# A recurrent-attention step with a new order on all five engines, its correction copied by ScalarE, and three expert sums in place of two

## The chip, the cores and the metric

The kernel runs on one core of one Trainium2 chip. The metric is device microseconds (us) for one execution. TensorE (PE) multiplies matrices into PSUM; VectorE (DVE) and ScalarE (ACT) read PSUM and SBUF; GpSimd (POOL) reads SBUF only; SyncE (SP) issues most of the DMAs. Each engine executes its own instructions in program order and waits on semaphores, so an instruction that waits holds up everything behind it on its engine.

## The reference

Two layers over 1024 tokens of width 256. The first is gated delta-rule attention (16 key heads, each with two value heads, all of size 128) and then a small MLP. The second is four-head softmax attention and then a mixture of 32 experts, four per token. What the change concerns:

```python
def step(state, xs):                      # per token, per value head
    q_t, k_t, v_t, g_t, b_t = xs
    state = state * jnp.exp(g_t)[..., None, None]
    kv = jnp.einsum('bhk,bhkv->bhv', k_t, state)
    delta = (v_t - kv) * b_t[..., None]
    state = state + jnp.einsum('bhk,bhv->bhkv', k_t, delta)
    out = jnp.einsum('bhk,bhkv->bhv', q_t, state)
...
mixed = jax.nn.silu(_causal_conv(mixed, conv_w))    # 4 taps, on q, k and v
o = o * jax.nn.silu(z); o = o * rsqrt(mean(o * o) + EPS) * norm_gamma
return o @ w_out
# experts: y[e] = (silu(x_e @ w_gate[e]) * (x_e @ w_up[e])) @ w_down[e]
# out[token] += weight * y[e][row of token]
```

## The kernel before

**The head steps.** `heads` computes the delta rule in chunks of 128 tokens: c = 0 to 7 for each key head. The program has 18 head steps, h = 0 to 17. Step h works on several heads at once: it scans head h-1, projects and convolves head h+1 (`p0` to `p7`, `base`, `tap`), inverts the chunk matrices of head h, and normalises and projects head h-2. Steps 2 to 14 are alike, with all of this work.

**One chunk of the scan** has three parts, (c, 0), (c, 1) and (c, 2). In part 0 PE multiplies the state S by keys (`ks`, L820) and queries (`qs`, L822), and DVE makes X from it (L1284). In part 1 PE multiplies X with the inverse Uf (`tx`, L833), and DVE copies the result from PSUM into Dl (L1289). In part 2 PE multiplies Dl with At (`o`, L839); ACT scales Dl into Dt (L1112); PE multiplies Dt with the keys (`su`, L845); DVE updates S (L1297) and finishes the output (L1309, L1311). So a chunk is a chain ks, X, tx, Dl, Dt, su, S that goes to and fro between the engines, and the next chunk starts from S.

**The order.** A step is a list of 23 quanta, the parts (0, 1), (0, 2), (1, 0) to (7, 2), numbered 0 to 22. Three tables written by hand, PE_PLAN, ACT_PLAN and DVE_PLAN, say which further work an engine does behind quantum k: the row `12: y6a/3 y6b/0` puts the products y6a and y6b behind quantum 12, into PSUM banks 3 and 0. Each engine runs its quantum and then its row, in this order:

```python
for h in STEPS:
    for k in range(NQUANTA):
        if h in SCAN:
            scan_quantum(h, *QUANTA[k])
        for name in dve_row(h, k):
```

SP and POOL have a fixed order per step, written as code.

**The inversion** goes around by HBM. PE makes key products (`kk0`, `kk1`, L799), ACT evicts them to `heads_kneg` (L1164), SP stores the 32x32 diagonal blocks to `kk_blocks` (L639, `key_block_stores`) and loads them regrouped into `heads_A` (L646, `load_key_blocks`). DVE computes block scales from it (`scales`, L1317 to L1325). POOL scales A (L1556) and eliminates in 31 rounds (L1566, L1569; `solve`). SP then stores the inverse (L734) and loads it into Uf (L742) in the next step, where DVE turns three blocks (`turn`, L1332); PE and ACT extend the inverse to 128 columns (`y6`, `u6`, `y7`, `u7`). POOL's rounds use the same tile as Y6 and start only when `u6a` is done.

**The experts** (`experts`, after everything else): PE computes expert e, DVE weights its 128 rows (L2252), POOL adds them with an indirect DMA into a sum in HBM (L2174). Adds to one sum follow each other, each waiting for the last to land; e alternates between SUMS = 2 sums. DVE's `places(e)` waits for the add of expert e-4. At the end SP loads the first sum in two halves (L2152) and the second in four quarters (L2156), DVE adds them to x (L2269, L2274), and SP stores x (L2161).

## Time and profile before

| | us |
|---|---|
| Median of 3 runs (lowest, highest) | 1622.71 (1614.81, 1622.80) |
| The profiled execution, its own time | 1607.9 |
| Its span in the trace | 1606.1 |
| Granted TensorE clock, mean, of full speed | 0.937 |
| Busy PE / DVE / ACT / POOL over the span | 1358.1 / 1028.1 / 757.8 / 749.6 |
| Steps 2 to 14, from 171.05 to 1075.91 | 904.86 |

Over the whole span PE is the busiest engine. A share of the span says little of what a stage waits for, so the rows below are taken from stages: from the 13 like steps, from one step (that with h = 10, from its first `tx` at 728.15 to the next step's at 797.04), and from the experts' end.

### The profile page before, as it was taken

Reading aid. Unit: us, or ns where it says so; the run is one execution under the profiler, and the core shown is the slowest. Engines: PE = TensorE matmul, PEld = TensorE weight load, DVE = VectorE, ACT = ScalarE, POOL = GpSimd, SP = SyncE. Lnnn points to the kernel's source line nnn. Section 1 sums busy time; section 2 is a strip of 40 time slices with the busy share of each in tenths; the row PEclk is TensorE's granted clock in tenths of the full one; section 3 lists DMA queues with packets and bytes.
Section 4 is the critical chain, followed back from the end, with each engine's and each line's share of the span. In section 5 each row is a group of like instructions: output and inputs, shape, how many; then the busy total and the mean of one; then the engine's idle time right before and its main releaser. Section 6 shows DMA issues by size and latency. Waiting matters only on the chain. (4 is left out here: it accounts for less than half of the span.)

```text
span 1606.1 us, 24958 instructions
## 1 busy us (share of the span) xinstructions
PE 1358.1 (85%) x8680; PEld 900.5 (56%) x8680; DVE 1028.1 (64%) x2086; ACT 757.8 (47%) x1787; POOL 749.6 (47%) x1226
## 2 busy tenths in 40 slices
PE   6686888979898897989889798898789689969994
PEld 3364655656565565656556565556554356644673
DVE  5765867778686777868777786776550256561353
ACT  3454645555554555555556564556442246311121
POOL 1774674746657474665747566472100000007254
PEclk9878999999999999999999999998999799979997
DMA  3513335444543444444344443435410390022387
GB/s 90 135 35 95 82 113 115 100 102 106 142 102 94 108 115 108 96 132 106 94 109 115 111 104 116 115 79 138 134 41 0 146 322 5 1 77 104 92 182 159
DMA packets 230989, 169.49 MB, mean 106 GB/s; under 512 B 163730, under 2 KB 200806, under 8 KB 228048
## 3 DMA queue, kind: packets, MB, share of 16 engines
q1 hardware_dynamic: 224720, 159.36, 36.9%
q0 software_dynamic: 6144, 8.53, 2.9%
q8 instruction: 70, 1.15, 0.3%
q14 instruction: 55, 0.45, 0.1%
HBM read 103.59 MB, written 64.65 MB: 105 GB/s over the span
## 5 line engine op out<-in xcount | busy, mean ns | idle before, releaser
L1273 DVE SCALAR_TENSOR_TENSOR heads_y<-psum_banks,gdn_conv_w,heads_y 128x1021 f32<-128x1021 f32 (+2 forms) x192 | 245.2, 1277 | 70.6 <-ACT heads_y L1087 69.0
L791 PE MATMUL psum_banks<-main_hT,gdn_w_in 128*128 128x512 f32 x512 | 265.8, 647 | 19.5 <-DVE heads_y L1273 13.1
L1566 POOL TENSOR_TENSOR heads_tmp<-heads_XT,heads_A 128x126 f32<-128x126 f32 (+22 forms) x496 | 189.1, 381 | 74.4 <-PE psum_banks L956 36.5
L1569 POOL TENSOR_TENSOR heads_XT<-heads_XT,heads_tmp 128x126 f32<-128x126 f32 (+22 forms) x496 | 200.9, 405 | 38.8
L1112 ACT ACTIVATE heads_Dt<-heads_Dl,heads_coef 128x128 f32<-128x128 f32 x224 | 77.6, 394 | 243.2 <-DVE heads_Dl L1289 242.8
L791 PEld LDWEIGHTS psum_banks<-main_hT,gdn_w_in 128*128 128x128 f32 x512 | 100.3, 208 | 114.8 <-issue 88.3
L1540 POOL TENSOR_TENSOR heads_og<-heads_og,heads_fac 128x512 f32<-128x512 f32 x60 | 60.5, 1039 | 144.8 <-DVE heads_fac L1343 144.8
L905 PE MATMUL psum_banks<-heads_w_z,main_hT 128*128 128x256 f32 x512 | 123.8, 386 | 0.0
L1105 ACT ACTIVATE heads_O<-psum_banks,heads_coef 128x128 f32<-128x128 f32 x224 | 69.9, 363 | 114.1 <-PE psum_banks L822 113.5
L2106 POOL DMA_INDIRECT expert_rows<-moe_rows,route_dest x32 | 31.4, 981 | 185.9 <-DVE route_dest L2085 176.5
L926 PE MATMUL psum_banks<-heads_ogT,heads_w_o 128*128 128x512 f32 x240 | 116.6, 608 | 1.0
L1123 ACT ACTIVATE heads_junk<-heads_og 128x128 f32<-128x128 f32 x256 | 78.0, 305 | 71.0 <-DVE heads_og L1311 66.5
L1551 POOL TENSOR_TENSOR heads_v_s<-heads_v_s,heads_k_root 128x2048 f32<-128x2048 f32 x16 | 58.2, 3638 | 98.5 <-DMA heads_v_s<-values_by_tokens 98.5
L905 PEld LDWEIGHTS psum_banks<-heads_w_z,main_hT 128*128 128x128 f32 x512 | 95.5, 194 | 11.4
L833 PEld LDWEIGHTS psum_banks<-heads_X,heads_Uf 128*128 128x128 f32 x448 | 63.5, 192 | 55.8 <-issue 28.7
L1289 DVE COPY heads_Dl<-psum_banks 128x256 f32<-128x256 f32 x128 | 53.1, 415 | 64.8 <-PE psum_banks L833 63.3
L1087 ACT ACTIVATE heads_y<-psum_banks,gdn_conv_w 128x1024 f32<-128x1024 f32 x64 | 71.4, 1116 | 43.0 <-PE psum_banks L791 42.7
L839 PE MATMUL psum_banks<-heads_Dl,main_lend 128*128 128x128 f32 x256 | 48.8, 319 | 48.0 <-DVE heads_Dl L1289 48.0
L833 PE MATMUL psum_banks<-heads_X,heads_Uf 128*128 128x128 f32 x448 | 74.1, 288 | 17.9 <-DVE heads_X L1284 17.6
L839 PE MATMUL psum_banks<-heads_Dl,heads_At 128*128 128x128 f32 x256 | 47.2, 310 | 48.6 <-DVE heads_Dl L1289 48.6
L845 PE MATMUL psum_banks<-heads_Dt,heads_k_tok 128*128 128x256 f32 x224 | 79.8, 441 | 4.5 <-ACT heads_Dt L1112 2.5
L820 PE MATMUL psum_banks<-heads_S,heads_kT 128*128 128x256 f32 x224 | 71.9, 403 | 10.9 <-DVE heads_S L1297 9.9
(280 smaller groups left out, 3002.8 us busy)
## 6 DMA issues: line engine op xcount, KB each, us to landing
values_by_tokens<-heads_v_s SPq DMA_DIRECT2D x64, 256.0 KB, 3.8
heads_v_s<-values_by_tokens SPq DMA_DIRECT2D x16, 1024.0 KB, 5.0
outputs_by_features<-heads_ogT SPq DMA_DIRECT2D x120, 128.0 KB, 2.3
heads_ogT<-outputs_by_features SPq DMA_DIRECT2D x30, 512.0 KB, 3.5
main_w_gu<-in_w_gu SPq DMA_DIRECT2D x4, 2816.0 KB, 20.8
gdn_w_in<-in_w_in SPq DMA_DIRECT2D x16, 512.0 KB, 4.4
heads_A<-kk_blocks SPq DMA_DIRECT2D x64, 128.0 KB, 2.6
keys_by_tokens<-heads_k_tok SPq DMA_DIRECT2D x64, 128.0 KB, 3.3
```

What stands on the lines that cost most here:

```text
L791: ins = pe.matmul(out[:, half * 512:(half + 1) * 512], w_in[:, kd_, j * P:(j + 1) * P], hT[:, kd_, half * 512:(half + 1) * 512], start=kd_ ...
L820: pe.matmul(flat(bank_a[:, 0:2]), kT[(h - 1) % 3][:, cs], flat(S[:]), start=True, stop=True).then_inc(a_full.sem, 1)
L833: ins = pe.matmul(bank_a[:, e], Uf[old][:, e * C + c], rhs, start=True, stop=True)
L839: ins = pe.matmul(bank_b[:, e], At[old][:, c * HD + e], Dl[:, e], start=True, stop=True)
L845: pe.matmul(flat(bank_a[:, 0:2]), k_tok[old][:, c], flat(Dt[:]), start=True, stop=True).then_inc(a_full.sem, 1)
L905: ins = pe.matmul(flat(bank[b][:, 2 * j:2 * j + 2]), hT[:, k, c * P:(c + 1) * P], w_z[:, k], start=k == 0, stop=k == KD - 1)
L926: ins = pe.matmul(flat(bank[b][:]), w_o[:, e, f], ogT[:, u // 2].rearrange("p q (c e) j -> p e c q j", e=HD)[:, e], start=e == 0, stop=e = ...
L1112: ins = act.activation(Dt[:, e], Dl[:, e], ACT.Copy, scale=coef[:, TAIL, h - 1, i:i + 1])
L1123: act.activation(junk[:], og[(h - 1) % 2][:, c * HD + e], ACT.Square, accum_out=ms[:, c * HD + e:c * HD + e + 1]).then_inc(sq_ready.sem, 1)
L1273: dve.scalar_tensor_tensor(y[j][:, shift:T], src[:, 0:T - shift], conv_w[:, head, j, t:t + 1], y[j][:, shift:T], ALU.mult, ALU.add).then_i ...
L1566: pool.tensor_tensor(tmp[:, 0:n, 0:m], bc_last(XT[:, 0:n, j], m), bc_mid(A0[:, j, j + 1:BLK], n), ALU.mult).then_inc(solve_step.sem, 1)
L1569: pool.tensor_tensor(XT[:, 0:n, j + 1:BLK], XT[:, 0:n, j + 1:BLK], tmp[:, 0:n, 0:m], ALU.add).then_inc(solve_step.sem, 1)
```

## The change

All tables of a steady step are filled anew, and the order of SP and of POOL becomes a table too, SP_PLAN and POOL_PLAN (POOL's order is the same as before). The PSUM banks of the four decay products are permuted, and some products change bank. The copy of the correction into Dl goes from DVE to ACT, in quantum part 1; ACT then makes Dt from the same PSUM bank and no longer from Dl. The semaphore for this copy is a new one, `dl_ready`. The experts' sums become three, each with its own zeroing, load and addition; the last of them is still taken in quarters. The tables for step 0 are as they were; those of step 1 are derived from the new ones.

```diff
-11: scales attn0
-12: attn1
-13: ot0
+11: attn0 ot0
+12: attn1 scales
...
+SP_PLAN = """kt_out inverse_out gates kt_in inverse_in values_out products_out values_in products_in
+outputs_out0 w_z outputs_in0 outputs_out1 outputs_in1 w_in w_o""".split()
+POOL_PLAN = """q_root pow norm0 norm1 norm2 norm3 scale solve""".split()
...
-                    pe.wait_ge(a_free.sem, a_free.done(h, f"tx{c}"))
+                    pe.wait_ge(dl_ready.sem, dl_ready.done(h, f"dl{c}"))
                     wait(pe, b_free, b_free.ahead(h, f"o{c}"))
...
                 elif part == 1:
+                    act.wait_ge(a_full.sem, a_full.done(h, f"tx{c}"))
+                    act.activation(flat(Dl[:]), flat(bank_a[:, 0:2]), ACT.Copy).then_inc(dl_ready.sem, 1)
                     if c < C - 1:
-                        act.wait_ge(a_free.sem, a_free.done(h, f"tx{c}"))
                         for e in range(HD):
                             i = c * HD + e
-                            ins = act.activation(Dt[:, e], Dl[:, e], ACT.Copy, scale=coef[:, TAIL, h - 1, i:i + 1])
+                            ins = act.activation(Dt[:, e], bank_a[:, e], ACT.Copy, scale=coef[:, TAIL, h - 1, i:i + 1])
                         ins.then_inc(dt_ready.sem, 1)
...
-                elif part == 1:
-                    dve.wait_ge(a_full.sem, a_full.done(h, f"tx{c}"))
-                    dve.tensor_copy(Dl[:], bank_a[:, 0:2]).then_inc(a_free.sem, 1)
...
-SUMS = 2
+SUMS = 3
...
+            for n, i in enumerate(ending[:-1]):
+                sp.wait_ge(s_summed[i], 16 * additions(i))
+                sp.dma_start(part[i][:], sums[i][0:T].rearrange("(t p) n -> p t n", p=P)).then_inc(s_part[n], 16)
+            last = ending[-1]
+            sp.wait_ge(s_summed[last], 16 * additions(last))
             for i in range(QUARTERS):
-                rows = sums[1][i * QT * P:(i + 1) * QT * P].rearrange("(t p) n -> p t n", p=P)
...
+            for n, i in enumerate(ending[:-1]):
+                dve.wait_ge(s_part[n], 16)
+                if n:
+                    dve.wait_ge(s_add, n)
+                dve.tensor_tensor(x[:], x[:], part[i][:], ALU.add).then_inc(s_add, 1)
```

On DVE, in the middle of a steady step, around the block scales (`heads_nd` to `heads_nd_t`), the order before was, from the state update of chunk 3 to the copy of chunk 4's correction:

```order
L1297 SCALAR_TENSOR_TENSOR heads_S<-heads_S,heads_coef,psum_banks 128x128 x2
L1309 TENSOR_TENSOR heads_og1<-psum_banks,heads_O1 128x256
L1311 TENSOR_TENSOR heads_og1<-heads_og1,heads_z 128x256
L1273 SCALAR_TENSOR_TENSOR heads_y1<-psum_banks,gdn_conv_w,heads_y1 128x1023
L1284 SCALAR_TENSOR_TENSOR heads_X<-psum_banks,heads_coef,heads_v_s1 128x128 x2
L1317 TENSOR_SCALAR heads_nd<-heads_A0 128x32
L1319 RECIPROCAL heads_rnd<-heads_nd 128x32
L1321 TENSOR_TENSOR heads_cb<-heads_rnd,heads_beta_rows 128x32
L1325 STREAM_TRANSPOSE heads_nd_t<-heads_nd 128x32
L1405 TENSOR_TENSOR main_lend<-psum_banks,heads_Dm 128x256 x4
L1289 COPY heads_Dl<-psum_banks 128x256
```

The change has there, from the turn of the inverse blocks (`heads_Xh`) on:

```order
L1342 STREAM_TRANSPOSE heads_Xh<-heads_Uf0 32x16x32 x3
L1307 SCALAR_TENSOR_TENSOR heads_S<-heads_S,heads_coef,psum_banks 128x128 x2
L1319 TENSOR_TENSOR heads_og1<-psum_banks,heads_O1 128x256
L1321 TENSOR_TENSOR heads_og1<-heads_og1,heads_z 128x256
L1297 SCALAR_TENSOR_TENSOR heads_X<-psum_banks,heads_coef,heads_v_s1 128x128 x2
L1415 TENSOR_TENSOR main_lend<-psum_banks,heads_Dm 128x256 x4
L1372 STREAM_TRANSPOSE heads_ogT<-heads_og0 128x8x4x32
L1415 TENSOR_TENSOR main_lend<-psum_banks,heads_Dm 128x256 x4
L1327 TENSOR_SCALAR heads_nd<-heads_A0 128x32
L1329 RECIPROCAL heads_rnd<-heads_nd 128x32
L1331 TENSOR_TENSOR heads_cb<-heads_rnd,heads_beta_rows 128x32
L1335 STREAM_TRANSPOSE heads_nd_t<-heads_nd 128x32
```

The scales have moved behind both masks `attn0` and `attn1` (into `main_lend`) and a transpose of outputs, the copy into Dl is gone from DVE, and the turn, moved from row 7 of the table to row 9, stands now between the last tap and the state update of chunk 3.

On SP, from the inverse blocks' store to the regrouped key blocks' load (`heads_A`), the order of a steady step before was:

```order
L734 DMA inverse_blocks<-heads_XT 1024x1x32
L694 DMA heads_k_tok<-keys_by_tokens 32x1024 [waits heads_keys_blocks_stored]
L694 DMA heads_k_tok<-keys_by_tokens 32x1024 x3
L742 DMA heads_Uf<-inverse_blocks 32x16x32 [waits heads_inverse_blocks_stored]
L742 DMA heads_Uf<-inverse_blocks 32x16x32 x3
L702 DMA values_by_tokens<-heads_v_s 32x4x512 [waits heads_values_by_tokens_loaded,heads_values_blocks_turned]
L702 DMA values_by_tokens<-heads_v_s 32x4x512 x3
L706 DMA heads_v_s<-values_by_tokens 128x2048 [waits heads_values_blocks_stored]
L639 DMA kk_blocks<-heads_kneg 32x8x32 [waits heads_kk_blocks_loaded,heads_bank0_free,heads_bank3_free]
L639 DMA kk_blocks<-heads_kneg 32x8x32 x3
L646 DMA heads_A<-kk_blocks 32x1024 [waits heads_kk_blocks_stored,heads_inverse_blocks_stored]
```

and is now:

```order
L666 DMA heads_row_to<-cum_dram 4x512 [waits heads_bank1_full]
L666 DMA heads_row_from<-cum_dram 4x512
L708 DMA heads_k_tok<-keys_by_tokens 32x1024 [waits heads_keys_blocks_stored]
L708 DMA heads_k_tok<-keys_by_tokens 32x1024 x3
L754 DMA heads_Uf<-inverse_blocks 32x16x32 [waits heads_inverse_blocks_stored]
L754 DMA heads_Uf<-inverse_blocks 32x16x32 x3
L716 DMA values_by_tokens<-heads_v_s 32x4x512 [waits heads_values_by_tokens_loaded,heads_values_blocks_turned]
L716 DMA values_by_tokens<-heads_v_s 32x4x512 x3
L653 DMA kk_blocks<-heads_kneg 32x8x32 [waits heads_kk_blocks_loaded,heads_bank3_free]
L653 DMA kk_blocks<-heads_kneg 32x8x32 x3
L720 DMA heads_v_s<-values_by_tokens 128x2048 [waits heads_values_blocks_stored]
L660 DMA heads_A<-kk_blocks 32x1024 [waits heads_kk_blocks_stored,heads_inverse_blocks_stored]
```

The two row loads (`gates`), which wait for the decay products in PSUM, stand now ahead of the loads of keys and of Uf, and the store of the key blocks ahead of the load of the values.

On ACT, between the corrections of chunks 2 and 3, the change has:

```order
L1121 ACTIVATE heads_Dl<-psum_banks 128x256
L1125 ACTIVATE heads_Dt<-psum_banks,heads_coef 128x128 x2
L1136 ACTIVATE heads_junk,heads_ms<-heads_og1 128x128 x2
L1146 ACT_TABLE_LOAD
L1146 ACTIVATE heads_Dm<-heads_Dm 128x512
L1158 ACTIVATE heads_w_o<-heads_w_o,gdn_gamma 128x512
L1177 ACTIVATE heads_kneg1<-psum_banks 128x512
L1099 ACTIVATE heads_y1<-psum_banks,gdn_conv_w 128x1024
L1146 ACTIVATE heads_Dm<-heads_Dm 128x512 x2
L1117 ACTIVATE heads_O1<-psum_banks,heads_coef 128x128 x2
L1177 ACTIVATE heads_kneg1<-psum_banks 128x512
L1121 ACTIVATE heads_Dl<-psum_banks 128x256
```

Before, the row L1145 (`heads_w_o`) stood behind chunk 3's Dt, four exponentials of `heads_Dm` stood here and not three, and no copy into Dl.

## Rows read from the trace of the kernel before

**Rows 1.** Windows: start:end, length, busy us of PE, PEld, DVE, ACT, POOL, clock, DMA.

```profile
171.05:1075.91 904.86, 794.49 (x5644) 537.58 (x5644) 675.65 (x1302) 504.31 (x1243) 550.39 (x943) 0.96 0.42 108
768.00:772.20 4.20, 4.20 (x11) 2.75 (x11) 3.32 (x9) 3.40 (x12) 3.26 (x3) 0.63 0.00 0
```

**Rows 2.** Waits of PE, 171.05 to 1075.91: us in total, times, longest us.

```profile
PE psum_banks L839 <- DVE heads_Dl L1289: 80.8, 39, 6.0
PE psum_banks L791 <- DVE heads_y L1273: 11.1, 13, 0.9
PE psum_banks L833 <- DVE heads_X L1284: 8.3, 13, 0.6
```

**Rows 3.** Waits of DVE, the same stretch.

```profile
DVE heads_nd L1317 <- DMA heads_A<-kk_blocks: 72.5, 13, 6.4
```

**Rows 4.** Timeline of PE in step 10: start, us, instructions, idle before.

```profile
728.15 0.61 PE L833 MATMUL psum_banks<-heads_v_s,heads_Uf 128*128 128x128 f32 x4
...
759.38 1.98 PE L791 MATMUL psum_banks<-main_hT,gdn_w_in 128*128 128x512 f32 x4 [0.86 <-DVE heads_y L1273]
...
768.00 1.22 PE L839 MATMUL psum_banks<-heads_Dl,heads_At 128*128 128x128 f32 x4 [5.12 <-DVE heads_Dl L1289]
...
772.20 0.59 PE L820 MATMUL psum_banks<-heads_S,heads_kT 128*128 128x256 f32 x2
...
773.15 0.21 PE L954 MATMUL psum_banks<-heads_Uf,heads_tmp 32*32 32x32 f32 x1
...
774.29 0.71 PE L833 MATMUL psum_banks<-heads_X,heads_Uf 128*128 128x128 f32 x4
...
797.04 0.61 PE L833 MATMUL psum_banks<-heads_v_s,heads_Uf 128*128 128x128 f32 x4
```

**Rows 5.** Timeline of DVE in step 10.

```profile
765.40 0.19 DVE L1317 TENSOR_SCALAR heads_nd<-heads_A 128x32 f32<-128x32 f32 x1 [5.56 <-DMA heads_A<-kk_blocks]
...
766.24 1.38 DVE L1405 TENSOR_TENSOR main_lend<-psum_banks,heads_Dm 128x256 f32<-128x256 f32 x4
767.53 0.41 DVE L1289 COPY heads_Dl<-psum_banks 128x256 f32<-128x256 f32 x1
```

**Rows 6.** Timeline of SP, steps 10 and 11: start, us of issuing, DMAs.

```profile
740.51 1.91 SPq L742 DMA_DIRECT2D heads_Uf<-inverse_blocks  x4
...
755.36 1.86 SPq L639 DMA_DIRECT2D kk_blocks<-heads_kneg  x4
760.75 2.57 SPq L646 DMA_DIRECT2D heads_A<-kk_blocks  x4
...
803.82 2.06 SPq L734 DMA_DIRECT2D inverse_blocks<-heads_XT  x2
```

**Rows 7.** Groups by line and shape, whole span: count, busy us, mean ns, idle before.

```profile
L1105 ACT ACTIVATE heads_O<-psum_banks,heads_coef 128x128 f32<-128x128 f32 x224 | 69.9, 363 | 114.1 <-PE psum_banks L822 113.5
L1133 ACT ACT_TABLE_LOAD x16 | 20.5, 1283 | 0.3
```

**Rows 8.** Timeline of ACT in step 10, the second eviction of key products.

```profile
753.43 0.62 ACT L1164 ACTIVATE heads_kneg<-psum_banks 128x512 f32<-128x512 f32 x1
```

**Rows 9.** Waits of PE in step 1, 96.9 to 171.05.

```profile
PE psum_banks L839 <- DVE heads_Dl L1289: 11.6, 4, 9.2
```

**Rows 10.** Timeline of the experts' end: POOL, SP and DVE.

```profile
1510.79 1.58 POOL L2174 DMA_INDIRECT expert_sum<-moe_ys,moe_place  x1 [24.53 <-DVE moe_ys L2252]
1513.26 1.58 POOL L2174 DMA_INDIRECT expert_sum<-moe_ys,moe_place  x1 [0.88 <-DVE moe_ys L2252]
...
1591.32 1.54 POOL L2174 DMA_INDIRECT expert_sum<-moe_ys,moe_place  x1 [1.10 <-DMA expert_sum<-moe_ys,moe_place]
...
1596.84 1.90 SPq L2156 DMA_DIRECT2D moe_part<-expert_sum  x4
...
1602.07 1.35 DVE L2274 TENSOR_TENSOR main_x<-main_x,moe_part 128x512 f32<-128x512 f32 x2 [0.92 <-DMA moe_part<-expert_sum]
```

More of the change, by code:

```diff
@@ L228 @@
 PE_PLAN = banked(rows("""
-0: z0/0
-1: p0/-1
-2: norm_q/0 p1/-1
-3: z1/3
-4: z2/2
-5: decay0/3 decay1/0 decay2/1 decay3/2
-6: p2/-1
+0: z0/0 p0/-1
+1: p1/-1
+3: z1/1
+4: norm_q/0 z2/2
+5: p2/-1
+6: decay0/3 decay1/2 decay2/0 decay3/1
 7: kk0/3 p3/-1
-8: kk1/0
+8: kk1/3
 9: attn0/1
-10: attn1/2
-11: p4/-1
-12: y6a/3 y6b/0
-13: p5/-1
-14: u6a/3 u6b/0
+10: p4/-1 attn1/2
+11: y6a/3 y6b/0
+12: p5/-1
+13: u6a/3 u6b/0
 15: z3/1
@@ L282 @@
 ACT_PLAN = rows("""
-0: z0 q_silu
-1: q_square v0_silu
-2: base0
-3: z1 v1_silu
-4: z2
-5: keys
-6: exp0 exp1
-7: exp2 exp3
-8: kk0 base1 kk1
-9: gamma
-12: norms y6a y6b
-14: base2 u6a u6b
-15: z3
-17: y7_0
-18: base3
-19: y7_1 u7_0
+0: q_silu z0 q_square
+1: base0
+3: v0_silu
+4: v1_silu keys z1 z2
+7: exp0 gamma kk0 base1 exp1 exp2
+8: kk1
+9: exp3
+10: y6a
+12: y6b
+13: base2 u6a norms
+15: u6b
+16: z3 y7_0
+18: base3 u7_0
+19: y7_1
 21: u7_1
@@ L322 @@
 DVE_PLAN = rows("""
-0: kt
-1: variance
-2: norm_q
-3: tap00 tap01
-4: tap02
-5: decay0 decay1 vt0
-6: decay2 decay3 vt1
-7: factors turn
-8: tap10
-9: tap11
-10: tap12
-11: scales attn0
-12: attn1
-13: ot0
-14: tap20
-15: tap21 tap22
-16: ot1
-18: tap30
-19: tap31
-20: inverse0 out0
-21: tap32 out1
-22: inverse1 out2 out3
+0: kt variance
+2: tap00 tap01
+3: tap02
+4: norm_q
+5: vt0 vt1 decay0
+6: decay1 decay2
+7: factors
+8: decay3 tap10
+9: tap11 tap12 turn
+11: attn0 ot0
+12: attn1 scales
+14: tap20 tap21
+15: tap22 ot1
+19: tap30
+20: out0 tap31
+21: inverse0 out1
+22: out2 tap32 inverse1 out3
 """)
@@ L368, in belongs @@
         return h == HK + 1
+    if name in ("w_in", "gates"):
+        return h + 2 < HK
+    if name == "w_z":
+        return h in SCAN and h < HK
+    if name in ("pow", "norm0", "norm1", "norm2", "norm3", "w_o") or name.startswith("outputs"):
+        return h in FINISH and h <= HK
     if name.startswith(("out", "gamma")):
@@ L372, in belongs @@
         return h in FINISH and h <= HK
-    if name.startswith(("kk", "p", "base", "tap", "keys", "norms", "scales")):
+    if name.startswith(("kk", "p", "solve", "base", "tap", "keys", "norms", "scales")):
         return h in AHEAD
@@ L400, in act_row, with sp_row, pool_row @@
     return [name for name in {0: ACT_FIRST, 1: ACT_SECOND, HK + 1: ACT_LAST}.get(h, ACT_PLAN)[k] if belongs(h, name)]
+def sp_row(h):
+    return [name for name in (SP_PLAN if h else SP_FIRST) if belongs(h, name)]
+def pool_row(h):
+    return [name for name in POOL_PLAN if belongs(h, name)]
 def dve_row(h, k):
@@ L719, in load_outputs, with transfer @@
                              og_cols[u].rearrange("a i q f -> (a i) (q f)")).then_inc(ot_loaded[u].sem, 16)
-            store_keys(0)
-            load_keys(0)
-            store_values(0)
-            load_values(0)
-            key_block_stores(0)
-            for h in STEPS:
-                if h in INVERT and h:
-                    store_keys(h)
-                if h in INVERT:
+            def transfer(h, name):
+                if name == "kt_out":
+                    store_keys(h)
+                elif name == "kt_in":
+                    load_keys(h)
+                elif name == "values_out":
+                    store_values(h)
+                elif name == "values_in":
+                    load_values(h)
+                elif name == "inverse_out":
                     wait(sp, a_full, a_full.base(h))
@@ L755, in _ @@
                     weights("w_z", w_z_ready, h, w_z)
-                if h + 2 < HK:
+                elif name == "gates":
                     b = bank_of(h, "decay3")
@@ L769, in _ @@
                     weights("w_o", w_o_ready, h - 1, w_o)
+            for h in STEPS:
+                for name in sp_row(h):
+                    transfer(h, name)
                 if h == HK - 1:
@@ L827, in scan_quantum @@
                         pe.wait_ge(uf_ready.sem, uf_ready.base(h) - 1 + c // 4)
-                    wait(pe, a_free, a_free.ahead(h, f"tx{c}"))
+                    wait(pe, a_free, a_free.done(h, f"ks{c}") if c else a_free.base(h))
                     if c == 0:
@@ L2134, in experts, with additions @@
     s_empty, s_place = a.sem("empty_rows_found"), a.sem("places_ready")
-    s_part, s_add, s_out = [a.sem(f"part{i}_loaded") for i in range(2 + QUARTERS)], a.sem("part_added"), a.sem("out_written")
-    HALFT, QT = NT // 2, NT // QUARTERS
+    s_part, s_add, s_out = [a.sem(f"part{i}_loaded") for i in range(SUMS - 1 + QUARTERS)], a.sem("part_added"), a.sem("out_written")
+    QT = NT // QUARTERS
+    ending = [(E - SUMS + n) % SUMS for n in range(SUMS)]
+    def additions(i):
+        return len(range(i, E, SUMS))
     with nc.Block() as block:
```

77 lines of the change are left out of this document (34 added, 43 removed).

## The prediction, made before the changed kernel ran

> **What bounds the kernel now.** I read the busy shares first, then the windows, then the waits of PE and of DVE over the 13 like steps, and then one step on PE, DVE and SP side by side. Steps 2 to 14 take 904.86 us, 69.60 each, more than half of the execution. PE is busy in 794.49 of it, so it stands still for 110.4, or 8.5 us a step [rows 1]. Three lines of its waits make up 100.2 of that, and one, the wait of `o` for DVE's copy Dl, 80.8 [rows 2]. The reader is to see that DVE does not make Dl slowly (0.41 us [rows 5]); it stands still itself, for 72.5 us, or 5.58 a step, at the block scales, until the regrouped key blocks have landed [rows 3]. In step 10 it waits 5.56 us until 765.40, finishes the scales at 766.24, masks, and copies Dl of chunk 4 only at 767.53 [rows 5]; PE has waited 5.12 us for it at 768.00 [rows 4]. Behind the stall the granted clock is 0.63 for 4.20 us [rows 1], so about a third of these, 1.5 us, is lost too. A step is thus PE's work, some 59 us, and a stall in the middle that a DMA sets.
>
> **The steps, part by part.** I write times as +us from a step's first `tx` (728.15 in step 10 [rows 4]).
>
> *When the blocks land.* Before, SP stored the key blocks at +27.2, issued their load at +32.6, and DVE's wait ended at +37.25 [rows 5, 6]. Now this store no longer stands behind the load of the values, but it still needs the second `kneg` eviction, in the same row 8 of ACT's table. That eviction ended at 754.05 [rows 8], 1.3 us ahead of the store: the gain lies between 0 and 1.3, and I take 1.0, so +36.3. The scales cost 0.84 us (765.40 to 766.24 [rows 5]). Then S of chunk 4 and `ks` of chunk 5 follow; with 0.7 for them, at +37.8. Before, this `ks` came at 772.20, +44.05 [rows 4].
>
> *When PE gets there.* What PE does up to there is to be had from step 10. It worked until its stall, 768.00 less 5.12, or +34.73 [rows 4]. In this lie 0.86 us of waiting at 759.38 [rows 4], and about 1.7 for X and Dl: the waits of [rows 2] come to 7.7 a step, less 5.1 and 0.86. That leaves 32.1 us of work. Into the time ahead of `ks` of chunk 5 now also come `o` and `su` of chunk 4 (0.45 and 0.5), p5 (1.85, by the 1.98 of p4 less its overlapped end) and u6a (774.29 less 773.15, 1.14 [rows 4]), because Dl of chunk 4 no longer stands behind the scales: 36.0.
>
> *The copy on ACT.* No row shows ACT copying 128x256 from PSUM; it lies between its 0.36 us for 128x128 [rows 7] and its 0.62 for 128x512 [rows 8], and I take 0.44, against 0.41 on DVE [rows 5]. A hop between two engines goes away ahead of Dt. What stands behind the copy in ACT's order is Dt and so `su`; what stands ahead of it is new. From Dl of chunk 2 up to Dl of chunk 3 ACT has Dl (0.44), six instructions of 128 columns (Dt, squares and O, 0.36 each: 2.2), a table load (1.28), six of 512 columns (0.6: 3.6) and a base of 1024 (0.93 by the same slope) [rows 7, 8]: 8.4 us, and then 0.44 for the copy itself. PE's work between the same points is three quanta of 23, 7.7 us of some 59, and a copy can start only some 0.6 behind its `tx`. So `o` of chunk 3 waits about 8.4 + 0.44 + 0.6 - 7.7, less the 0.4 that `tx` itself takes: 1.4 us, a new stall. With less of this on PE's path it would be 0, with one more base ahead of the copy 2.4. The sum takes 1.4: PE is at `ks` of chunk 5 at +37.4. The two paths, +37.8 and +37.4, meet there; the later one counts.
>
> *The rest of the step.* From `ks` of chunk 5 to the next step's first `tx` took 797.04 less 772.20, 24.84. u6a (1.14) has moved ahead of it: 23.7. Row 14 of PE's table now has nothing between `ks`/`qs` and `tx`, so X (0.6 and its latencies) is no longer covered: plus 0.4; about 0.5 of old waits in this stretch goes. So 23.6, and the step takes 61.4, against 68.89 in step 10: 7.5 less. The mean step is 0.7 longer than step 10, all of it in waits, of which I give back a little: 7.7. Thirteen steps: 100.
>
> *Where the wait goes, and what is late next.* The turn now stands ahead of S of chunk 3 on DVE and waits for Uf. POOL's elimination ends as late as the scales make it: before, the scales ended at 766.24 and SP stored the inverse at 803.82, 37.6 later [rows 5, 6]. With the scales at +37.2 this is +74.8, or +13.4 in the next step. SP then waits for the decay products (behind quantum 6 of 23, about +17) to load the rows (1), and issues the keys (2.6, as four loads take) and Uf (1.9); four loads landed 2.1 behind their issue (763.33 to 765.40) [rows 5, 6]: Uf is there near +25. DVE comes to the turn with quantum 10, near +26. This is hidden by 1 us only; each us beyond costs one on PE, since S, and so `ks` of chunk 4, is queued behind it. The sum takes nothing for it.
>
> *The other steps.* Step 1 waited 11.6 us for Dl [rows 9]; its tables come from the new ones, with the scales as late in them: 8 back, bounds 3 and 11. Steps 15 and 16 have no scales; there the missing hop in 15 chunks and the shorter DVE queue give 2, bounds 0 and 6. The other tables, the permuted banks among them, add no instruction: each new owner of a bank comes after the eviction that frees it by the two orders, the nearest (kk1 behind kk0 in bank 3) by less than 1 us; so nothing, bounds 0 and 1 a step, the latter within the range.
>
> *The experts.* The adds begin at PE's pace, 1510.79 to 1513.26, 2.47 us [rows 10]. By 1591.32 the 31st interval had come to 80.53 in all, 2.60 each, the last held by the add before it in its sum [rows 10]. Three sums leave each add 7.4 us, and the last one lands 5.5 us after its issue (1591.32 to 1596.84 [rows 10]), so the adds keep pace: 31 times 2.47 is 76.6, and PE's last two experts, with less to do, give some 2 more: 6 us earlier. Given back: one more load of 1 MB and one more addition (four quarters take 2.7, by 1.35 for two [rows 10]) next to the last loads, about 3. I take 3 gained, bounds 6 gained and 4 lost (adds that take as much longer as there are more of them). Zeroing a third sum is hidden by attention's products.
>
> The Trainium skill speaks against this part: "DMA: Bandwidth & Descriptors", section "Issuing engines are not separate DMA queues", says that all DMAs of a core run on the same 16 engines and interleave, whichever engine began them. By that a third add in flight brings no new engine, and if the adds were limited by the engines' work the sum would lose the 3 and the term would be 3 to 4 lost. The rows do not decide it: the last add, almost alone, takes 5.5 us, which is latency rather than sharing.
>
> **The sum.** 100 + 8 + 2 + 3 = 113. From the profiled execution's own 1607.9 us (span 1606.1) this leaves 1494.9. The three timed runs have their median at 1622.71, 1.0092 times as much; scaled, the forecast is 1509.
>
> **The rivals.**
> - *The wait only moves.* The blocks land no sooner than +37.25 and Uf misses the turn by some 2 us, or ACT's new stall is 2.4 and another like it comes: a step of 65.5. For it speaks that two DMA chains keep their length while the step shrinks, and that hidden by 1 us is not much; against it that neither chain has a transfer more. 13 times 4.1 more: 1494.9 + 53 = 1548, scaled 1562.
> - *All of it is hidden.* The blocks land by +35, ACT keeps up: PE's 36.0 and 23.2 make 59.2 a step. 13 times 2.2, with step 1 and the experts at their better bounds, is 35 less: 1460, scaled 1473. For it speaks only that the key blocks' store has one thing less ahead of it.
> - *Slower: the inversion becomes a loop that sets the step.* Scales, elimination, store, gates, keys, Uf, turn, S of chunk 3, `ks`, masks, scales: all of it is now in series on DVE's order, and SP puts the gates, which wait for PE, ahead of Uf. The change loses from the point where Uf lands 9.7 us later than I reckon, near +35 (1 us of slack and 113/13 = 8.7). At 12 us late a step takes 72.5: 1494.9 + 143 = 1638, scaled 1653. Against it: SP's waits between these DMAs are known and short.
> - *It doesn't do what it says.* S of chunk 4 is still behind the scales, and the blocks land later by the time that PE is now earlier at kk1: the step stays near 69, the result near 1615.
>
> **How the numbers follow.** Forecast 0.60 (steps of 60.5 to 63.5, 1497 to 1537); the wait moves 0.18; all hidden 0.14; slower 0.05; no effect 0.03. The range 1466 to 1575 takes in the first three. About 0.5% is what a measurement of this kernel can tell from none: faster 0.92, same 0.03, slower 0.05.
>
> **What would show it.** In the changed profile the wait at the first scales line should be 1 to 2.5 us a step and no longer be followed by a wait of PE's `o` on chunk 4; PE's wait for Dl should now name ACT, at chunk 3, near 1.4; PE's next wait should be `ks` for S, below 2.5; the clock in steps should be 0.98 or more; the turn should not wait. A DVE wait at the turn of more than 1 us, or scales that wait 5, makes the forecast wrong; an experts' end that is not shorter by 1 to 6 us from the first add to the last DMA makes the term of the experts wrong.

## The result: 3.2% faster, less than half of the forecast gain

The changed kernel takes 1566.14 us (median of 4 runs, 1565.12 to 1568.13), the kernel before 1618.76 on the same chip: a ratio of 0.9677, 95% interval 0.9641 to 0.9713. The gain is 52.6 us; forecast were 113. The profiled execution took 1565.12 us, its span is 1563.3. In the tables below the medians are of all runs of a kernel and the ratios of its fast ones; one run, of `both`, was slow (1527.12).

The kernel before was later profiled a second time (below), so the spans can be cut at the same places of both. All in us, from the timelines:

| from ... to | before | before, again | after | change forecast |
|---|---|---|---|---|
| start, first `tx` of step 2 | 171.05 | 171.88 | 164.42 | -8 |
| 13 steps | 904.86 | 902.30 | 870.22 | -100 |
| step 15 | 54.38 | 54.38 | 49.26 | -2 with step 16 |
| step 16, first row of the scatter | 315.13 | 320.38 | 310.14 | |
| scatter, first expert add | 65.37 | 75.56 | 75.35 | 0 |
| first add, end | 95.31 | 97.00 | 93.91 | -3 |

Only the second line is far off: 66.94 us a step instead of 61.4 to 61.9. In the windows of the changed kernel's trace (columns as in [rows 1]) PE is busy for 786.53 us in the 13 steps, and the clock fell: 0.93, against 0.96 before.

```profile
164.42:1034.64 870.22, 786.53 (x5644) 546.71 (x5643) 675.67 (x1198) 520.81 (x1348) 553.70 (x946) 0.93 0.43 112
943.60:950.00 6.40, 5.26 (x14) 3.91 (x15) 6.30 (x10) 3.35 (x12) 6.09 (x6) 0.50 0.00 0
```

The waits of PE and DVE over the same steps answer to [rows 2, 3]:

```profile
PE psum_banks L832 <- DVE heads_S L1307: 53.8, 13, 5.6
PE psum_banks L845 <- DVE heads_X L1297: 11.5, 26, 1.5
PE psum_banks L803 <- DVE heads_y L1286: 9.7, 13, 0.8
PE psum_banks L851 <- ACT heads_Dl L1121: 6.5, 13, 0.8
DVE heads_nd L1327 <- DMA heads_A<-kk_blocks: 36.6, 12, 3.8
```

The wait for Dl has gone, as meant (80.8 to 6.5, and it names ACT). In its place `ks` waits for S, 4.1 us a step: S of chunk 4 is behind the scales on DVE, and these are late. Step 13 (first `tx` at 902.50, the origin of its +us) shows it. First SP, then DVE, then POOL, then PE, as in [rows 4 to 6]:

```profile
920.37 0.55 SPq L666 DMA_DIRECT2D heads_row_to<-cum_dram  x1
...
921.53 3.22 SPq L708 DMA_DIRECT2D heads_k_tok<-keys_by_tokens  x4
924.79 2.02 SPq L754 DMA_DIRECT2D heads_Uf<-inverse_blocks  x4
926.91 3.05 SPq L716 DMA_DIRECT2D values_by_tokens<-heads_v_s  x4
930.07 3.23 SPq L653 DMA_DIRECT2D kk_blocks<-heads_kneg  x4
933.34 0.45 SPq L720 DMA_DIRECT2D heads_v_s<-values_by_tokens  x1
934.55 1.71 SPq L660 DMA_DIRECT2D heads_A<-kk_blocks  x4
```

```profile
941.14 1.78 DVE L1327 TENSOR_SCALAR heads_nd<-heads_A 128x32 f32<-128x32 f32 x1 [3.82 <-DMA heads_A<-kk_blocks]
...
943.45 0.20 DVE L1335 STREAM_TRANSPOSE heads_nd_t<-heads_nd 128x32 f32<-128x32 f32 x1
943.58 0.56 DVE L1307 SCALAR_TENSOR_TENSOR heads_S<-heads_S,heads_coef,psum_banks 128x128 f32<-128x128 f32 x2
944.06 0.42 DVE L1319 TENSOR_TENSOR heads_og<-psum_banks,heads_O 128x256 f32<-128x256 f32 x1
944.51 1.73 DVE L1321 TENSOR_TENSOR heads_og<-heads_og,heads_z 128x256 f32<-128x256 f32 x1
```

```profile
939.24 3.64 POOL L1561 TENSOR_TENSOR heads_v_s<-heads_v_s,heads_k_root 128x2048 f32<-128x2048 f32 x1 [11.61 <-DMA heads_v_s<-values_by_tokens]
943.61 2.35 POOL L1566 TENSOR_TENSOR heads_A<-heads_A,heads_cb 128x1024 f32<-128x1024 f32 x1 [0.73 <-DVE heads_cb L1331]
```

```profile
944.20 1.22 PE L832 MATMUL psum_banks<-heads_S,heads_kT 128*128 128x256 f32 x2 [5.42 <-DVE heads_S L1307]
```

The blocks' load is issued at 934.55, right behind the 1 MB load of the values. DVE's wait for it ends at 941.14, +38.6. The first scales instruction then takes 1.78 us, in [rows 5] 0.19, and ends with POOL's multiply of the values (939.24 + 3.64 = 942.88). PE stands for 5.42 us, and from 943.60 to 950.00, the end of the stall and what follows, the granted clock is 0.50, the lower of its two levels (1.2 GHz). The last view of the two kernels gives the DMAs of the whole run, with their median time from issue to landing (KB and us); first before, then after:

```profile
heads_A<-kk_blocks SPq DMA_DIRECT2D x64, 128.0 KB, 2.6
kk_blocks<-heads_kneg SPq DMA_DIRECT2D x64, 32.0 KB, 4.3
```

```profile
heads_A<-kk_blocks SPq DMA_DIRECT2D x64, 128.0 KB, 4.9
kk_blocks<-heads_kneg SPq DMA_DIRECT2D x64, 32.0 KB, 2.0
```

The store of the blocks lands 2.3 us sooner, their load 2.3 later: the values' load has moved from ahead of the one to ahead of the other.

### The profile page after: what moved, and what is told of

The parts are those of the page before. It is cut to its first block and busy times, and to the rows that moved or that the text cites. A ratio compares the mean times of both kernels' runs of the same rounds, so it can differ in the third digit from the quotient of the medians.

```text
span 1563.3 us, 24959 instructions
## 1 busy us (share of the span) xinstructions
PE 1346.6 (86%) x8680; PEld 908.1 (58%) x8680; DVE 1024.9 (66%) x1958; ACT 778.6 (50%) x1915; POOL 751.7 (48%) x1226
## 5 line engine op out<-in xcount | busy, mean ns | idle before, releaser
L803 PE MATMUL psum_banks<-main_hT,gdn_w_in 128*128 128x512 f32 x512 | 247.1, 608 | 16.5 <-DVE heads_y L1286 10.4
L803 PEld LDWEIGHTS psum_banks<-main_hT,gdn_w_in 128*128 128x128 f32 x512 | 93.8, 193 | 97.3 <-issue 77.1
L917 PE MATMUL psum_banks<-heads_w_z,main_hT 128*128 128x256 f32 x512 | 146.6, 438 | 0.0
L1307 DVE SCALAR_TENSOR_TENSOR heads_S<-heads_S,heads_coef,psum_banks 128x128 f32<-128x128 f32 x192 | 57.2, 339 | 98.6 <-PE psum_banks L857 98.2
L917 PEld LDWEIGHTS psum_banks<-heads_w_z,main_hT 128*128 128x128 f32 x512 | 108.7, 223 | 21.8 <-issue 6.2
L1297 DVE SCALAR_TENSOR_TENSOR heads_X<-psum_banks,heads_coef,heads_v_s 128x128 f32<-128x128 f32 x224 | 67.8, 344 | 61.8 <-PE psum_banks L832 61.7
L1121 ACT ACTIVATE heads_Dl<-psum_banks 128x256 f32<-128x256 f32 x128 | 49.2, 385 | 109.9 <-PE psum_banks L845 109.7
L832 PEld LDWEIGHTS psum_banks<-heads_S,heads_kT 128*128 128x128 f32 x224 | 42.0, 204 | 101.3 <-DVE heads_S L1307 70.0
L845 PE MATMUL psum_banks<-heads_X,heads_Uf 128*128 128x128 f32 x448 | 82.5, 311 | 17.8 <-DVE heads_X L1297 17.8
L1321 DVE TENSOR_TENSOR heads_og<-heads_og,heads_z 128x256 f32<-128x256 f32 x128 | 78.8, 616 | 4.4
```

The costliest lines, as they stand in the source:

```text
L803: ins = pe.matmul(out[:, half * 512:(half + 1) * 512], w_in[:, kd_, j * P:(j + 1) * P], hT[:, kd_, half * 512:(half + 1) * 512], start=kd_ ...
L832: pe.matmul(flat(bank_a[:, 0:2]), kT[(h - 1) % 3][:, cs], flat(S[:]), start=True, stop=True).then_inc(a_full.sem, 1)
L845: ins = pe.matmul(bank_a[:, e], Uf[old][:, e * C + c], rhs, start=True, stop=True)
L917: ins = pe.matmul(flat(bank[b][:, 2 * j:2 * j + 2]), hT[:, k, c * P:(c + 1) * P], w_z[:, k], start=k == 0, stop=k == KD - 1)
L1321: dve.tensor_tensor(mine, mine, gate, ALU.mult).then_inc(og_ready.sem, 1)
```

## The experiments

The theory: the blocks land late by SP's new order, and the scales are slowed beside POOL's multiply. The first rival: the step is as long as PE's order makes it. Step times are means of the 13 steps; the ratio is to the kernel before, with its 95% interval.

| kernel | median us | ratio | step |
|---|---|---|---|
| after | 1566.14 | 0.9677 (0.9641 to 0.9713) | 66.94 |
| blocks_first | 1505.13 | 0.9293 (0.9251 to 0.9335) | 61.53 |
| gates_late | 1521.10 | 0.9398 (0.9331 to 0.9465) | 62.86 |
| both | 1500.50 | 0.9259 (0.9225 to 0.9293) | 60.90 |
| old_blocks | 1488.15 | 0.9174 (0.9140 to 0.9209) | 60.77 |
| sp_as_before | 1511.60 | 0.9340 (0.9322 to 0.9358) | 62.59 |
| sp_padded | 1521.02 | 0.9389 (0.9367 to 0.9411) | 62.83 |
| dl_on_dve | 1590.64 | 0.9818 (0.9785 to 0.9851) | 67.81 |
| copy_alone | 1598.17 | 0.9867 (0.9852 to 0.9883) | 67.79 |
| both_mul_later | 1496.84 | 0.9243 (0.9225 to 0.9261) | 61.28 |
| gates_late_mul_later | 1496.63 | 0.9240 (0.9198 to 0.9282) | 61.27 |
| two_sums | 1574.87 | 0.9712 (0.9667 to 0.9756) | 66.70 |
| pieces | 1528.49 | 0.9430 (0.9401 to 0.9458) | 63.84 |
| both_pieces_later | 1489.27 | 0.9193 (0.9163 to 0.9224) | 60.66 |

### Two words swapped in SP's table

```diff
-SP_PLAN = """kt_out inverse_out gates kt_in inverse_in values_out products_out values_in products_in
+SP_PLAN = """kt_out inverse_out gates kt_in inverse_in values_out products_out products_in values_in
```

> SP issues the load of the key blocks ahead of the load of the values (1 MB); nothing else differs from the changed kernel, whose step takes 66.94 us, with the scales' wait ending at +38.6 and 6.6 us after the blocks' load began to be issued (4.65 in the kernel before). Theory 'late landing' (the blocks land late because SP's new order has the gates and the values' load just ahead of them): the load is issued 1.2 us earlier and does not share the DMA engines with 1 MB, so the wait ends 2 to 3 us earlier, the step takes 64 to 65, the whole 25 to 40 us less than the changed kernel's 1566. Rival 'PE's own order' (the step is as long as PE's work and its many small waits make it, the late scales are beside the path): within 8 us of 1566. Rival 'two engines in one memory' (POOL's multiply of the values slows DVE's scales): the scales still take over 2 us where the multiply, now later, falls on them, and half of the gain is lost.

61 us less, where the theory had asked for 25 to 40; the rival that PE's order sets the step is out. SP, DVE and POOL in step 13 (first `tx` at 839.27):

```profile
871.42 1.71 SPq L660 DMA_DIRECT2D heads_A<-kk_blocks  x4
873.18 0.43 SPq L720 DMA_DIRECT2D heads_v_s<-values_by_tokens  x1
```

```profile
875.37 0.19 DVE L1327 TENSOR_SCALAR heads_nd<-heads_A 128x32 f32<-128x32 f32 x1 [1.28 <-DMA heads_A<-kk_blocks]
...
876.22 0.56 DVE L1307 SCALAR_TENSOR_TENSOR heads_S<-heads_S,heads_coef,psum_banks 128x128 f32<-128x128 f32 x2
```

```profile
879.21 3.64 POOL L1561 TENSOR_TENSOR heads_v_s<-heads_v_s,heads_k_root 128x2048 f32<-128x2048 f32 x1 [14.30 <-DMA heads_v_s<-values_by_tokens]
```

The wait ends 3.95 us after the load's issue instead of 6.59, and the scales have POOL to themselves, since the values now land behind them. The clock in the steps is 0.98. Step 13 flatters the landing, though: over the 13 steps the scales start at +36.77 for +37.65, only 0.9 sooner, because the blocks' load is itself issued 1.5 us later (+32.43 for +30.91). The scales take 0.92 for 2.47, and the stretch behind `ks` of chunk 5 takes 23.30 for 26.27. So the expectation had the right move and the wrong shares: of the 5.4 us a step, 0.9 are the landing, 1.6 the multiply that no longer falls on the scales, and 3.0 what follows. In the whole kernel the 13 steps gain 70.4 us, of which step 15 gives back 10.1 (59.41 for 49.26).

### The gates behind w_z, and both moves

In `gates_late` the word `gates` moves behind `w_z` and the loads stay as in the changed kernel; `both` has the two moves.

> SP issues the gates' rows behind the weights w_z, as in the kernel before, instead of ahead of the keys; the values' load still stands ahead of the blocks'. Theory 'late landing': SP no longer waits 8.0 us a step for the decay products (96.0 in 12) ahead of keys, inverse, values and blocks; the blocks' store can move up to the second eviction of the negated keys, 2.9 us earlier in step 13, so the scales' wait ends 1.5 to 3 us earlier: 15 to 40 us less than 1566. Rival 'PE's own order': within 8 us of 1566.

> Both moves on SP at once: blocks' load ahead of the values' load, gates behind w_z. Theory 'late landing': the scales' wait ends at +34 to +36 instead of +38.6, the step takes 62 to 64, the whole is 40 to 65 us below 1566 and the clock in the steps rises from 0.92 to 0.96 or more. Rival 'two engines in one memory': the scales still take over 2 us against 0.84 in the kernel before, and the step stays above 64.5. Rival 'PE's own order': within 10 us of 1566.

With the gates late the load goes out at +27.9 in the mean, DVE no longer waits (the scales start at +34.84, by DVE's own order), and still they take 2.1 us, the first of them 1.41: the second half of the theory. It gains 45 us, a little more than the 15 to 40 expected. With both moves the step is 60.90, below the 62 to 64 expected; the clock is 1.00, PE's 5643 matmuls take 744.28 us, 42 less than in the changed kernel. So some 3.2 us of its 66.94 are clock. `both` and `blocks_first` can't be told apart by their intervals.

### The landing taken away

From step 2 on `old_blocks` works on the blocks of the head before, so its outputs are other ones.

```diff
-SP_PLAN = """kt_out inverse_out gates kt_in inverse_in values_out products_out values_in products_in
+SP_PLAN = """kt_out inverse_out gates kt_in inverse_in products_in values_out products_out values_in
...
```

The load then waits for the stores of the step before, and the next store for the load.

> From step 2 on the key blocks are loaded right behind the keys and the inverse, before the step's own blocks are stored: the scales and the elimination work on the blocks of the head before, so the outputs are other ones, while every instruction and transfer stays. The blocks are there long before DVE asks for them. This shows what a step costs when the landing is taken away as a cause. Theory 'late landing': no wait of DVE at the scales, no stall of PE's ks of chunk 5 above 1.5 us, step 60 to 62, the whole 1480 to 1505. Rival 'PE's own order': the step stays at 64.5 or more, the whole above 1530. Rival 'two engines in one memory': scales wait for nothing but still take 2 us or more.

As expected: DVE never waits for the blocks, PE not for S, and the step is 60.77 (one of the 13 took 68.66, the others 58.8 to 61.0). The tables could give what was forecast.

### What SP's new order cost, and what ScalarE's copy brought

`sp_as_before` has the changed kernel's other tables and SP's old order; `dl_on_dve` the changed kernel's tables and the copy on VectorE; `copy_alone` the old tables on all engines, with the copy on ScalarE and three sums.

```diff
-                    act.activation(flat(Dl[:]), flat(bank_a[:, 0:2]), ACT.Copy).then_inc(dl_ready.sem, 1)
...
+                    dve.tensor_copy(Dl[:], bank_a[:, 0:2]).then_inc(dl_ready.sem, 1)
```

(This is from `dl_on_dve`; there ACT's Dt reads Dl again.)

> SP's order of a step is that of the kernel before (values stored and loaded ahead of the blocks, gates behind w_z); all else is the changed kernel. Theory 'late landing', with its second half, that POOL's multiply of the values slows DVE's scales where they meet (the first scales instruction took 0.19 us apart from it, 0.7 to 2.7 beside it): the values turn at +17 to +19, so their load can go out near +22 and POOL is done with them by +32; the blocks' load goes out near +28, the scales start at +34.75 by DVE's own order, take 0.9, and PE reaches ks of chunk 5 at +36 to +37: step 59 to 60, the whole 1470 to 1490. Rival 'the loop of the inversion binds' (as in the kernel with both moves, where the inverse is stored at +18.4 of the next step): step 60.5 to 61.5, 1495 to 1508. Rival 'the values' load ahead of the blocks costs by itself': the scales start after +36, 1505 or more.

> The changed kernel with the copies Dl on VectorE again (Dt reads Dl, as before); all tables stay. Theory 'late landing': in the new tables the scales stand behind Dl of chunk 4 in any case, and their end sets PE's ks of chunk 5; the step stays 66 to 68. The gap from scatter to first add goes back to 24.5, since ScalarE's and VectorE's programs have their old lengths: 1550 to 1570. Rival 'the copy on ScalarE is what gains': PE's o waits 1 us or more at each of eight chunks, step 69 or more, 1585 or above.

> The kernel before's tables on all five engines, with the copies Dl on ScalarE and the three sums of the experts. Theory: the stall at the scales stays on DVE (5.6 us) but PE's o of chunk 4 no longer stands behind it; PE waits for S at ks of chunk 5 instead, from about +40 instead of +44.7. Step 65 to 67, 45 to 60 us less in the steps, 10 lost at the scatter: 1565 to 1585. Rival 'only the tables gain': step 69 to 70, 1615 or more. Rival 'only the copy gains': like the changed kernel or better, below 1560.

SP's old order under the new tables is 54.5 us faster than the new one: the refilled SP table is the part of the change that loses. It isn't the best one either: the scales start at +37.24, where DVE's own order has them at +34.8. The third of the rivals had the number (after +36, 1505 or more), but not the cause. The blocks' store does land late beside the values (3.8 us), yet DVE waits for the blocks in none of the 13 steps. What is late is DVE itself. POOL's multiply now comes earlier and falls on the gate multiply of the chunk ahead of the scales, 0.42 us alone; DVE, then POOL, in step 13:

```profile
885.59 3.21 DVE L1321 TENSOR_TENSOR heads_og<-heads_og,heads_z 128x256 f32<-128x256 f32 x1
```

```profile
884.88 3.64 POOL L1561 TENSOR_TENSOR heads_v_s<-heads_v_s,heads_k_root 128x2048 f32<-128x2048 f32 x1 [4.16 <-DMA heads_v_s<-values_by_tokens]
```

In the 13 steps it takes 2.90 us in the mean (2.12 to 3.54) and ends 0.28 behind POOL's multiply each time; PE's waits for X, the next thing on DVE, come to 40.8 us (14.9 in `both`).

The copy brings 24.5 us in the new tables (1590.6 to 1566.1), 11.2 of them in the 13 steps and 5.6 in step 15. In the old ones it brings 22.4 with the third sum (1620.54, the kernel before on the same chip, to 1598.17). I had expected less of it in the first and more in the second. With the old tables the stall only changes its name: the waits of PE there are

```profile
PE psum_banks L841 <- DVE heads_S L1316: 60.5, 13, 5.3
```

4.7 us a step, and the clock stays at 0.93.

### The multiply moved, and cut

`both_mul_later` and `gates_late_mul_later` put POOL's multiply of the values inside the elimination, behind four of its rounds or none; `pieces` is the changed kernel with the multiply in eight instructions, `both_pieces_later` the first of these in eight pieces, one behind each of eight rounds.

```diff
-                pool.tensor_tensor(mine, mine, root, ALU.mult).then_inc(v_scaled.sem, 1)
+                for i in range(NB * HD):
+                    ins = pool.tensor_tensor(mine[:, i:i + 1], mine[:, i:i + 1], root[:, i:i + 1], ALU.mult)
+                ins.then_inc(v_scaled.sem, 1)
```

> SP's order as in the kernel with both moves (step 60.9: the values land late, POOL multiplies them at +40.9, 3.2 us after the scales ended, and only then begins the elimination, whose result is stored at +18.4 of the next step; DVE's factors and PE's y then wait). Here POOL multiplies the values inside the elimination, after four of its rounds. Theory 'the elimination's start is what is left': it starts at once behind the scales, the inverse is stored at +14 to +16, keys, Uf, values and blocks follow earlier, the scales start at +34.75 by DVE's own order, step 59 to 60, the whole 12 to 25 us below the 1500.5 of the kernel with both moves. Rival 'two engines in one memory': the multiply now falls on DVE's X and taps and costs as much: 1495 to 1510.

> SP's order as in the kernel with the gates late alone (1521, step 62.86: the scales start at +34.84 without waiting, but take 2.1 us instead of 0.9, the first of them 1.41 instead of 0.19, while POOL multiplies the values beside them). Here POOL multiplies the values behind the scaling of the blocks, before the first round. Theory 'two engines in one memory': the scales take 0.9 to 1.0 us, PE is at ks of chunk 5 at +36 to +36.7, step 60 to 61.5, 1480 to 1500. Rival 'the scales' length is beside the path': within 6 us of 1521. Rival 'the multiply takes its toll wherever it is': the scales are short, X of chunk 5 or S gets longer by 1 to 2 us, 1510 to 1525.

> The changed kernel with POOL's multiply of the values (128x2048, 3.6 us) cut into eight of 128x256; all else is the same. Theory 'held for the length of one instruction': DVE's first scales instruction (1.75 us in the mean of 13 steps, 0.19 without POOL beside it) waits for one piece at most, 0.3 to 0.7 us; the scales take 1.2 to 1.8 instead of 2.5, step 65 to 66, the whole 1540 to 1558. Rival 'both engines slow each other in proportion': the first instruction still takes over 1.2 us, the whole is within 6 us of 1566.

> SP's order with both moves, POOL's multiply of the values inside the elimination as in the kernel at 1496.8 (step 61.28, in which DVE's X of chunk 6 comes 1.2 us late beside the multiply), but in eight pieces, one after each of eight rounds. Theory 'held for the length of one instruction': no X is more than 0.6 us late, step 59.7 to 60.6, the whole 1478 to 1490. Rival 'in proportion': the pieces cost what the whole costs: 1492 to 1500.

Moving the multiply behind the scales gives `gates_late` 24.5 us, as expected: its scales take 0.91 us. For `both`, where it never fell on the scales, it gives no more than 4, where the theory wanted 12 to 25: PE's waits for X, which DVE makes, grow from 14.9 to 30.1 us in the 13 steps instead. Cutting it settles how the two engines meet. In step 13 of `pieces` (first `tx` at 875.03) DVE and POOL:

```profile
913.78 0.19 DVE L1327 TENSOR_SCALAR heads_nd<-heads_A 128x32 f32<-128x32 f32 x1 [3.93 <-DMA heads_A<-kk_blocks]
```

```profile
912.64 4.96 POOL L1562 TENSOR_TENSOR heads_v_s<-heads_v_s,heads_k_root 128x256 f32<-128x256 f32 x8 [12.47 <-DMA heads_v_s<-values_by_tokens]
```

The pieces run on both sides of it, and it takes 0.32 in the mean of 13 steps (0.19 to 0.65), against 1.75 beside the whole multiply. One piece takes 0.62 (4.96 by eight). So DVE is held until POOL's running instruction ends; slowing in proportion is out. The blocks land as late as ever here (+37.78, 37.65 in the changed kernel), and yet the kernel gains 37.6 us, more than the 8 to 26 expected: 1.4 a step in the scales, and 1.2 in PE's own work (770.93 us for 786.53) at a clock of 0.95. `pieces` thus takes away most of the hold and leaves the landing, `gates_late` takes away the wait for the landing (45.0 us) and leaves most of the hold: each half of the theory is worth some 40 us without the other. `both_pieces_later` is the fastest version that works on its own blocks: 9 of its 13 steps take 60.0. It is 76.9 us faster than the changed kernel (1566.14 less 1489.27), 0.9193 (0.9163 to 0.9224) of the kernel before. Its interval ends just below that of `both_mul_later` (0.9225 to 0.9261) and overlaps that of `gates_late_mul_later`, so what the cutting adds to the moving is small: 7.6 and 7.4 us by the medians. Its windows:

```profile
166.56:955.12 788.56, 750.20 (x5644) 522.08 (x5644) 664.60 (x1198) 520.20 (x1348) 557.53 (x1028) 0.99 0.48 124
```

### The ten microseconds in front of the first add

In every kernel with the change 34.3 to 37.7 us pass between the last row of the scatter and the first add; the first profile of the kernel before has 24.5. My theory was an instruction load that stands behind the scatter and falls at another place, because two engines' programs have other lengths.

```diff
+            for _ in range(128):
+                act.wait_ge(loaded["ident"], 16)
...
+            for _ in range(128):
+                dve.wait_ge(loaded["ident"], 16)
```

> As the kernel with SP's old order, with 128 waits more on ScalarE and 128 on VectorE ahead of the feed-forward stage, all on a semaphore that has long been reached: the program of each of the two engines is longer ahead of the routing stage, nothing else differs. In every kernel with the Dl copies on ScalarE the first expert add comes 34.3 to 34.7 us after the last row of the scatter, 24.5 in the kernel before, with ScalarE and VectorE idle for 8 to 17 us, and a load of instructions in the trace as they go on, right after the scatter. Theory 'instruction load behind the scatter': with another length of program the load falls elsewhere; the gap is 24 to 26 and the whole 7 to 10 us shorter than without the waits (or, if 64 instructions don't reach, 34.5 again). Rival 'something else of the changed kernel' (sums, banks, clock): the gap stays 34.5.

> The changed kernel with two sums of the experts instead of three. For the end of the kernel: from the first add to the end 93.9 us with three, 95.3 in the kernel before with two; with two 95 to 96. For the 10 us lost between the scatter and the first add (34.5 against 24.5 in the profile before), which neither another length of ScalarE's and VectorE's programs nor the old tables took away: theory 'third sum': 24.5 again, the whole 8 us below 1566. Rival 'not of this change' (the profile of the kernel before is the one without the loss, its timed runs have it): 34.5 stays, the whole within 4 us of 1566.

> The kernel before, profiled a second time. Its first profile was of an execution of 1607.9 us, 11 to 15 below the median of its timed runs. Theory 'not of this change': this profile has 34.5 us between the last row of the scatter and the first add, ScalarE and VectorE idle for 8 to 17 us in it, and is 10 us longer, near 1618. Rival 'of this change': 24.5 again.

The gap stayed in `sp_padded` (34.6; the waits themselves cost 9 us ahead of the scatter), in `dl_on_dve` (34.6), with the old lengths, and in `two_sums` (34.7). The second profile of the kernel before settles whose it is. POOL there, then in the changed kernel:

```profile
1524.50 1.58 POOL L2174 DMA_INDIRECT expert_sum<-moe_ys,moe_place  x1 [34.65 <-DVE moe_ys L2252]
...
1606.63 1.54 POOL L2174 DMA_INDIRECT expert_sum<-moe_ys,moe_place  x1 [1.16 <-DMA expert_sum<-moe_ys,moe_place]
```

```profile
1469.39 1.58 POOL L2192 DMA_INDIRECT expert_sum<-moe_ys,moe_place  x1 [34.53 <-DVE moe_ys L2270]
...
1545.04 1.54 POOL L2192 DMA_INDIRECT expert_sum<-moe_ys,moe_place  x1 [0.30 <-issue]
```

The 10 us are not of the change: the first profile ([rows 10], 24.53) was of an execution without them. They account for most of what its 1607.9 us lay below the median of the timed runs. What makes ScalarE and VectorE stand there for 8 to 17 us stays open.

The same rows show the third sum. From first add to end: 95.3 and 97.0 us before, 93.9 after, 98.1 with two sums in the changed kernel. It brings 1.4 to 4.2; the times of the whole (1566.1 and 1574.9) point the same way, but their intervals overlap.

## Why the prediction was wrong, point by point

- **"When the blocks land" failed first.** I saw that the store "no longer stands behind the load of the values" and asked what would hold the store. I did not ask what the values' load stands ahead of now: the blocks' load. I had +36.3; the mean of the 13 steps is +37.65, against +37.35 before. The load is issued 2.0 us earlier (+30.91 for +32.90) and takes 2.3 longer. By itself this is 1.35 us a step, a quarter of what was missing.
- **"The scales cost 0.84 us" failed.** They took 2.47 in the mean: the values land when the blocks do, so POOL's multiply falls on the scales. I had moved POOL's work nowhere in my sum, though the transfer that starts it was moved. With the landing left as late as it was and only the multiply cut (`pieces`), 37.6 us come back.
- **The clock followed.** I gave back the "1.5 us" that the slow clock costs behind a stall. The stall stayed (4.1 us a step for S), and so did the slow stretch. From `ks` of chunk 5 to the next `tx` came to 26.27 for the forecast 23.6; in `both`, with a stall of 0.8, it is 22.66. PE's matmuls in this stretch are busy for 25.65 us at a clock of 0.86 here, and for 22.41 at 1.00 there. The sum closes: 1.35 + 1.63 later at the scales, 0.15 less at S, 2.67 behind them, in all 5.5 a step over the forecast's 61.4.
- **PE's side held.** I had PE at `ks` of chunk 5 at +37.4, with 1.4 for a wait on ACT; it got there at +36.3 (944.20 less 5.42 less 902.50), with 0.5 for ACT: the term for the copy was too large by 0.9, the place right. A step of 61.4 was there to be had: 61.53 with the two loads swapped, and a whole of 1505.13 against the forecast 1509.
- **The turn** did not wait, as forecast. **Step 1** gave 3.9 to 4.0 of the 8 (70.24 us from its first `tx` for 74.16 and 74.28), inside the bounds; the rest of the first line of the table lies ahead of it, where two kernels with one order differ by 2 us (its first `tx` at 96.58 in `sp_as_before`, 94.54 in `sp_padded`), so that it came near the forecast -8 by luck. **Steps 15 and 16** gave 5.1 and, up to the feed-forward stage, 4.9 (7.7 by the second profile of before), over my bound of 6. **The experts** gave 1.4 to 4.2; I had 3. The rule of the Trainium skill that spoke against them ("DMA: Bandwidth & Descriptors", "Issuing engines are not separate DMA queues") did not decide there: with three sums the adds keep PE's pace (75.65 us from the first to the last, 82.13 in the second profile of before, 82.67 with two sums in the changed kernel). It fits the blocks, where I had not applied it: beside the values' load theirs took 4.9 us for 2.6.
- **The rival that came true** is "the wait only moves", at 65.5 a step and 1562, with a chance of 0.18. Its half on the blocks ("no sooner than +37.25") is what happened; its half on the turn is not. That its 1562 lies so near is in part luck: its step was 1.4 us short, and the hold by POOL is not in it.

## What to carry to other kernels

When a transfer is moved in a queue, write down both neighbours: what no longer waits for it, and what now does. Then ask which engine starts when it lands, and which instruction of another engine runs at that moment: in the changed kernel POOL's multiply fell on the scales, in `sp_as_before` on a gate multiply, and PE waited for both. A stall of PE that stays can keep a slow clock behind it: with the change, waits for S of 4.1 us a step went with a clock of 0.93, 2.9 with 0.95, and 0.8 with 1.00. The length of the wait is not all of it: the kernel before waited 6.2 a step for Dl at 0.96.
